# A window-attention block and a channel attention on one core: token deviations by quarter, slices turned around the third down-product, moments one product later, the attention's end in another order

## The reference, cut to what matters

```python
# first block: shifted-window attention (12 heads of 8, windows of 8 x 8), then an MLP
x = shortcut + window_attention(layernorm(x))          # over channels, per pixel
h = _layernorm(x, norm2_g, norm2_b)                    # (x - mu) * rsqrt(var + eps) * g + b, per pixel
h = jax.nn.gelu(h @ fc1_w + fc1_b, approximate=False)  # 96 -> 384
x = x + (h @ fc2_w + fc2_b)                            # 384 -> 96
# second block: channel attention; statistics over a whole image
mu = jnp.mean(x, axis=(1, 2, 3), keepdims=True)
var = jnp.mean((x - mu) ** 2, axis=(1, 2, 3), keepdims=True)
xn = (x - mu) * jax.lax.rsqrt(var + EPS) * ln_g + ln_b
Q, K, V = _proj(xn, ...)                               # 12 x 12 per head, then a 3 x 3 depthwise convolution
logits = jnp.einsum('bhnc,bhnd->bhcd', K, Q) / alpha
out = jnp.einsum('bhnc,bhcd->bhnd', V, softmax(logits))
return jnp.einsum('bcij,oc->boij', out, w_f) + b_f + xn
```

## Time and profile before

| | |
|---|---|
| time, median of 3 runs | 512.71 us (511.64 to 522.3) |
| the profiled execution's own time | 512.89 us |
| its span in the profile | 511.1 us |
| PE busy | 488.5 us, 96% of the span |
| DVE, ACT, POOL busy | 371.9, 292.6, 190.3 us |
| PE on the chain that ended last | 36% of the span, the largest share |
| mean granted clock of PE | 0.983 of full speed |

### The profile page before, as it was taken

One profiled execution on the slowest core, in us unless ns is written; L12 is line 12 of the kernel. 1 busy time (PEld: TensorE's weight loads), 2 busy tenths in 40 slices (PEclk: granted clock), 3 DMA queues, 4 the chain that ended last, 5 costly groups with the idle time before them and its releaser, 6 DMA issues. The chain is left out here.

```text
span 511.1 us, 22940 instructions
## 1 busy us (share of the span) xinstructions
PE 488.5 (96%) x8866; PEld 312.7 (61%) x8866; DVE 371.9 (73%) x1016; ACT 292.6 (57%) x740; POOL 190.3 (37%) x222
## 2 busy tenths in 40 slices
PE   7999999999999999999888997889999999999996
PEld 7777777777777777777643332325565556555563
DVE  2599999999999999998775362356776565565543
ACT  2477788777787777886564353143444444444332
POOL 8543444443434434344250413035325332332300
PEclk8899999999999999999999999889999999999998
DMA  4211011111011110100033142356543444434311
GB/s 81 64 35 33 21 26 49 31 31 27 21 31 31 31 31 21 40 1 3 3 74 74 32 99 53 82 130 150 137 128 98 127 110 117 114 103 130 106 38 34
DMA packets 41180, 32.55 MB, mean 64 GB/s; under 512 B 19240, under 2 KB 36776, under 8 KB 41128
## 3 DMA queue, kind: packets, MB, share of 16 engines
q1 hardware_dynamic: 36872, 25.36, 19.4%
q0 software_dynamic: 3584, 5.72, 5.1%
q10 hardware_dynamic: 672, 0.75, 0.5%
HBM read 18.36 MB, written 7.13 MB: 50 GB/s over the span
## 5 line engine op out<-in xcount | busy, mean ns | idle before, releaser
L379 POOL TENSOR_TENSOR scores<-scores,peak 128x768 f32<-128x768 f32 x64 | 94.2, 1472 | 129.8 <-DVE peak L548 129.8
L1033 POOL DMA_DIRECT2D x_stack<-padded_x x96 | 52.2, 547 | 95.8 <-PE ps_hidden L1552 63.6
L442 ACT COPY probs_t<-ps_probs 128x768 f32<-128x768 f32 x64 | 51.1, 798 | 40.4 <-PE ps_probs L702 40.3
L540 DVE TENSOR_TENSOR scores<-ps_scores,bias 128x768 f32<-128x768 f32 x64 | 61.3, 958 | 5.6 <-PE ps_scores L692 3.8
L548 DVE TENSOR_REDUCE peak<-scores 128x12 f32<-128x768 f32 x64 | 61.0, 953 | 2.4
L715 PE MATMUL ps_out<-v_blocks,probs_t 128*64 128x54 f32 x1536 | 57.1, 224 | 1.0 <-ACT out_t L447 0.9
L715 PEld LDWEIGHTS ps_out<-v_blocks,probs_t 128*64 128x64 f32 x1536 | 50.2, 138 | 12.3 <-issue 12.2
L436 ACT ACTIVATE scores<-scores 128x768 f32<-128x768 f32 x64 | 54.2, 847 | 1.5 <-POOL scores L379 1.5
L702 PE MATMUL ps_probs<-ident,scores 128*128 128x128 f32 x384 | 54.3, 277 | 0.0
L1140 ACT ACTIVATE hidden<-ps_hidden,fc_b_folded 128x512 f32<-128x512 f32 x44 | 26.6, 688 | 39.3 <-PE ps_hidden L1469 38.8
L1552 PE MATMUL ps_turn<-x_stack,conv_w 40*32 40x256 f32 x1536 | 48.8, 379 | 0.0
(11 more groups left out here) (159 smaller groups left out, 850.9 us busy)
## 6 DMA issues: line engine op xcount, KB each, us to landing
x_stack<-padded_x POOLq DMA_DIRECT2D x96, 54.0 KB, 2.7
x_stack<-padded_x SPq DMA_DIRECT2D x96, 54.0 KB
padded_x<-x_pad SPq DMA_DIRECT2D x26, 121.5 KB, 2.6
x_sliced<-stream SPq DMA_DIRECT2D x48, 64.0 KB, 2.0
stream<-y_sliced SPq DMA_DIRECT2D x48, 64.0 KB, 2.0
out<-out_sb SPq DMA_DIRECT2D x32, 96.0 KB, 2.2
x_now<-in_x SPq DMA_DIRECT2D x32, 72.0 KB, 1.8
stream<-in_x SPq DMA_DIRECT2D x32, 72.0 KB, 1.9
```

Of the source, the lines that this page charges most:

```text
L379: nc.gpsimd.tensor_tensor(sc, sc, peak[:, par, p, :].unsqueeze(2).to_broadcast((128, HEADS, WN)), ALU.subtract).then_inc(s["shifted"], 1)
L442: nc.scalar.copy(probs_t[:, :], ps_turned).then_inc(s["turned_copied"], 1)
L540: nc.vector.tensor_tensor(scores[:, par, p, :].rearrange("p (g c) -> p g c", g=NG), ps_scores[:, :, 0:GROUP * WN], bias[:, p, :].rearrange ...
L1033: engine.dma_start(x_stack[64 * half + i * HC:64 * half + (i + 1) * HC, slot, :, :], rows).then_inc(landed[slot], 16)
```

## The change

- **Attention's end.** PE turns chunks 4 and 5 ahead of the first fold, 6 ahead of the second, 7 after it, and does the third fold after the loop, where the 16 filling products stood. ACT takes its copies in that order. The three slice copies move from DVE to ACT, and the load of the GELU table from the end of this stage to the start of the next.
- **Deviations by quarter.** `quarter_deviation` makes shift and power for one quarter (4 columns) right ahead of that quarter's scaling, in place of one of 16 columns ahead of four scalings.
- **Turned slices.** `turn_back(g + 1, 0)` and `(g + 1, 1)` stand ahead of `down(g - 1, 2)`, `turn_back(g + 1, 2)` behind it. The turns of the third weight and of the final weight, and their copies on DVE, move from group 0 to group 1, behind its first up-product.
- **Moments.** In the last group `sum_means`, `center_means` and `sum_spreads` stand one product later; the inverse roots come in three parts of 2, 4 and 10 images, and `take_gain` of images 0 and 1 waits for the first, of 2 to 5 for the second. All six `start_image` stand behind the last GELU and ahead of the table load.

```diff
@@ window attention, ACT
             if is_image(t, B - 1):
+                copy_first(0)
                 copy_fold(0)
+                copy_first(1)
                 copy_fold(1)
-                for k in range(QUARTERS, 2 * QUARTERS):
-                    copy_tokens(nc, act, m, s2, k, by_blocks(first_homes[k - QUARTERS]))
-                    if k == QUARTERS + 1:
-                        copy_fold(2)
-                token_deviation(nc, act, m, s2, 1)
-                nc.scalar.preload_act_table_set("gelu_and_others")
+                copy_first(2)
+                copy_fold(2)
...
+        def copy_slice(c):
+
+            act.wait_ge(s2["turned_ready"], c + 1)
+            nc.scalar.copy(m["normed2"][:, c, :], ps_slices[c]).then_inc(s2["normed_ready"], 1)
...
         led_image_loop(act, step)
+        copy_slice(0)
+        copy_first(3)
+        copy_slice(1)
+        token_deviation(nc, act, m, s2, 1)
+        copy_slice(2)
...
@@ window attention, PE
             if last:
+                turn_first(QUARTERS)
+                turn_first(QUARTERS + 1)
                 fold_fc1(0)
+                turn_first(QUARTERS + 2)
                 fold_fc1(1)
-                for k in range(QUARTERS, 2 * QUARTERS):
-                    turn_first(k)
-                fold_fc1(2)
+                turn_first(QUARTERS + 3)
...
-        fill(nc, ps_out[0:C, 0, 0:C], blank[:, :], 16)
+        fold_fc1(2)
         for c in range(SLICES):
             turn_first_slice(c)
...
+def quarter_deviation(nc, pool, m, s, g, r, exponent, shifted):
+
+    n = (g - 2) * QUARTERS + r
+    pool.wait_ge(s["spread_ready"], (g * QUARTERS + r + 1) * BLOCKS)
+    need(pool, s["quarter_ready"], n)
+    need(pool, s["scaled_ready"], (g - 1) * QUARTERS + r + 1)
+    nc.gpsimd.tensor_scalar(m["log_var2"][:, r, :], m["spread_mlp"][:, r, :, 1], EPS, None, ALU.add).then_inc(shifted, 1)
+    pool.wait_ge(shifted, n + 1)
+    nc.gpsimd.tensor_tensor(m["rstd2"][:, r, :], m["log_var2"][:, r, :], exponent[:, 0:1].to_broadcast((128, BLOCKS)),
+                            ALU.pow).then_inc(s["quarter_ready"], 1)
...
@@ MLP, POOL
         for g in range(2, GROUPS):
-            token_deviation_by_power(nc, pool, m, s, g, exponent, variance_shifted)
             for r in range(QUARTERS):
+                quarter_deviation(nc, pool, m, s, g, r, exponent, variance_shifted)
                 scale_tokens(nc, pool, m, s, g, r)
...
+            for first, last in ((0, 2), (2, AHEAD), (AHEAD, EARLY)):
+                at = batch * EARLY
+                nc.gpsimd.tensor_tensor(moments[:, at + first:at + last, 0], spread2[:, first:last, 1],
+                                        exponent[0:C, 0:1].to_broadcast((C, last - first)), ALU.pow).then_inc(deviations_set, 1)
...
@@ MLP, ACT
-            if g == LAST:
-                act.wait_ge(cleared, CLEARED)
-                start_image(0)
-                start_image(1)
             gelu(g, 2)
+        act.wait_ge(cleared, CLEARED)
+        for t in range(AHEAD):
+            start_image(t)
         nc.scalar.preload_act_table_set("natural_log_exp_and_others")
-        for t in range(2, AHEAD):
-            start_image(t)
...
@@ MLP, DVE
+            if g == 1:
+                copy_weights(2, 2)
+                copy_final()
...
             if g == 0:
-                for place, kind in enumerate((1, 0, 2)):
-                    copy_weights(place, kind)
-                copy_final()
+                copy_weights(0, 1)
+                copy_weights(1, 0)
...
@@ MLP, PE
             if last:
-                sum_spreads(0)
+                sum_means(0)
             if g > 0:
                 down(g - 1, 1)
+            if last:
+                sum_spreads(0)
             up(g, 2)
-            if g > 0:
-                down(g - 1, 2)
+            if more:
+                turn_back(g + 1, 0)
+                turn_back(g + 1, 1)
             if g == 0:
-                turn_back(1, 0)
-                turn_back(1, 1)
                 turn_weights(0, 1)
                 turn_weights(1, 0)
-                turn_back(1, 2)
-                turn_weights(2, 2)
-                nc.tensor.transpose(ps_final, w["final"][:, :], ident[0:C, 0:C]).then_inc(weights_turned, 1)
-            elif more:
-                for c in range(SLICES):
-                    turn_back(g + 1, c)
+            else:
+                down(g - 1, 2)
+            if more:
+                turn_back(g + 1, 2)
```

More of the change, by code:

```diff
@@ L837, in measure_tokens @@
     dve.wait_ge(s["stats_ready"], (k + 1) * BLOCKS)
-    need(dve, s["rstd_ready"], k // QUARTERS)
+    need(dve, s["rstd_ready"], min(k // QUARTERS, 2))
+    need(dve, s["quarter_ready"], k - 3 * QUARTERS + 1)
     for b in range(BLOCKS):
@@ L1256, in center_means @@
             dve.wait_ge(means_summed, batch + 1)
-            need(dve, deviations_set, batch)
+            need(dve, deviations_set, batch * PARTS_OF_BATCH)
             nc.vector.tensor_reduce(mean_sum[:, :], sums, AX_X, ALU.add).then_inc(moments_set, 1)
@@ L1349, in _ @@
                 add_residual(g - 1, 0)
-            if last:
-                center_means(0)
             if 1 < g < LAST:
@@ L1511, in _ @@
             up(g, 0)
+            if g == 1:
+                turn_weights(2, 2)
+                nc.tensor.transpose(ps_final, w["final"][:, :], ident[0:C, 0:C]).then_inc(weights_turned, 1)
             if later:
@@ L1515, in _ @@
                 down(g - 1, 0)
-            if last:
-                sum_means(0)
             if later:
```

36 lines of the change are left out of this document (13 added, 23 removed).

## The result

The changed kernel takes 498.91 us, median of 4 runs (499.01, 507.1, 497.83, 498.81), against 515.92 us for the kernel before, median of 4 (511.64 to 522.3): a ratio of 0.9696 with a 95% interval from 0.9631 to 0.9761, faster. The ratio leaves out the execution of 507.1 us, which lies apart from the others; the experiments show what such an execution of this kernel is. The profiled execution took 499.01 us for a span of 497.2 us, at a mean granted clock of 0.994.

The account below looks back on a forecast made before the run. PE was taken as the path, with holes, up to image 2's products of the channel attention. Savings of 1.7 + 1.0 + 3.2 + 7.5 = 13.4 us from 512.9 us gave 499.5 us, range 497 to 503.5 us.

Parts of the forecast that it names:

- Part 1: Attention's end: new order of turns, folds and copies brings the last slice copy from 257.36 to 255.7 us, saving 1.7 us.
- Part 2: Group 0: PE's 1.42 us wait for turned conv weights goes as the turns move behind the next up-product, saving 1.0 us.
- The 0.4 us that were to stay: Group 0: of PE's 1.42 us wait, 0.4 us stay because the next up-product needs a GELU that ended at 268.77 us.
- Part 3: Groups 2 and 3: deviations by quarter and turned slices ahead of the down-product remove PE's waits, saving 3.2 us.
- the margin of 0.2 us: Group 3: POOL's chain ends at 306.7 us, PE asks at 306.88 us; a small power over 1.0 us costs time.
- Part 4: Last group and first images: later moment products and pads behind the GELU bring image 2 from 49.2 to 41.7 us, saving 7.5 us.
- their 0.4 us hole: Last group: PE is done at 8.3 us, moments are ready at 8.7 us, so it waits 0.4 instead of 3.19 us.
- 0.5 us for the taps to land: Between PE's last down-product at 25.6 us and the first taps' product: a wait of 0.5 us.
- SP ends last, PE waits 1.2 us: At image 2: SP's chain allows its products at 41.7 us, PE gets there at 40.5 us and waits 1.2 us.
- First rival: POOL's quarters: the small power keeps its price, every quarter costs 4.2 us, 515.0 us in all; chance 0.08.
- Second rival: MLP's start: without filler PE stands about 2 us and the clock falls, costing 1.7 us, 501.2 us; chance 0.17.
- Third rival: SP's gathers wait the full 3.4 us, image 2 comes 2.9 us later and half clock adds 1.7 us: 504.1 us; chance 0.15.

## Why the prediction was right

The forecast was 499.5 us, the profiled execution took 499.01 us. From the last heads to image 2 the sum said 13.4 us and the traces say 13.10 us (1.56 + 1.42 + 2.65 + 7.47); 1.56 us of luck in the start and 0.74 us lost at the kernel's end belong to neither.

- **Part 1,** 1.7 us: 1.56 us. The new order does it; moving the copies to ACT costs 0.16 us, which the bounds held and the sum had not named.
- **Part 2,** 1.0 us: 1.03 us, namely 1.42 us less the 0.39 us that the moved turns take in the next stretch (268.50 to 268.89). The 0.4 us that were to stay are the 0.45 us ahead of 265.71.
- **Part 3,** 3.2 us: 3.04 us (2.65 + 0.39). The power of 4 columns is 1.04 us and not 0.93 us, just over the point from which it was to cost something, but it stays hidden: shift and hand-overs are 0.07 us shorter, and of the margin of 0.2 us 0.05 us are left. With 2.93 us for 16 columns this is (2.93 - 1.04) / 12 = 0.16 us a column and 0.41 us besides. The three inverse roots of 2, 4 and 10 columns lie near the same line, at 0.69, 1.00 and 1.95 us. The Trainium skill, GPSIMD: programming the Q7 cores, section SBUF Data Layout, says that a read hands a core one vector of 16 lanes from 16 partitions, from which the prediction took a price by the column; the trace agrees for all but the 0.41 us.
- **Part 4,** 7.5 us: 7.47 us, but this is luck, two errors that cancel. PE was through 24.87 us after the first up-product, not 25.6 us, because the moments were ready at 8.14 us (311.36 + 2.71 - 305.93) and their 0.4 us hole did not come. Against that, the step "0.5 us for the taps to land" was 1.63 us, and the stretch from there to image 2 was 15.23 us and not 14.4 us, 0.40 us of it idle. The step "SP ends last, PE waits 1.2 us" failed: image 2's products have no wait ahead of them, since SP's last joins are issued by 34.34 us (331.78 + 8.49 - 305.93) and not by 37.2 us. SP matters one step earlier, with its gathers of the first taps behind its joins.
- **First rival,** the small power keeps its price: it doesn't. The run with one power isn't that case, but it shows what late scaled tokens cost: 9.9 us in two groups, with half clock behind the second hole only, where the rival had it behind both.
- **Second rival,** clock at the MLP's start: real, and seen in one of twelve profiles that have this order without filler there. The other eleven had the same hole of 1.4 to 1.7 us and kept 1.00. The Trainium skill, TensorE: Matmul & The Clock Gate, section What's actually happening, which the prediction cites there, says that half rate is the default and that activity lifts it. It follows neither from that nor from these traces that filler is needed in a stand of this length.
- **Third rival,** SP: the pads did leave ACT ahead of its table load, and twelve gathers took 5.17 us, so its wait of 3.4 us did not come.

What the prediction lacked is the third hole. It asked of three places whether the clock would fall and priced 1.7 us. At the first taps it saw 0.5 us of waiting, where 1.64 and 2.32 us came in the two profiles of the changed kernel, and with the longer one a loss of 8.3 us. The forecast is that of the executions in which this doesn't happen; that three of the first four runs were such is luck as far as the runs tell, for in the repeated runs the same kernel had a median of 507.68 us, outside the range.

## What to carry to other kernels

When an edit makes PE arrive earlier at a stage whose data come by transfers, the wait moves to the first use of that data: ask who issues these transfers and what is queued ahead of them. Here it was enough to move the one producer (a 0.41 us copy on ACT) that starts their chain; moving SP's transfers too gained nothing more. A kernel can have two times, so repeat the runs before believing a median of four, and compare the profiles of a short and a long execution stretch by stretch. Work split by columns is worth it even at a start-up price per piece, where the pieces let the order of the consumer change.

## What the hardware showed that I had not expected

- At the start of the channel attention the clock fell in all six profiles in which PE had waited 1.95 us or longer for the first taps (1.95, 2.32, 2.78, 2.79, 2.84, 3.91 us), and in none of the other six (1.64, 0.55 us and less). It stayed at 0.50 for 20.5 us in five of them and 23.9 us in the sixth, with PE busy for all of it, where the falls in the MLP lasted 3.4 or 6.8 us. In the MLP a hole of 1.69 us was followed by half clock in one profile and one of 3.41 us wasn't, so the length by itself isn't a rule.
- Two executions of one kernel, equal to 0.01 us in the stretches before, differed by 1.0 us in the time SP took to issue the same twelve joins (7.76 and 8.76 us), all of it in the twelfth (0.59 and 1.71 us), with the DMA engines' share at 0.52 and 0.57 during the joins; 8.3 us hung on it.
- A power on POOL took 2.93 us for 128x16 elements and 1.04 us for 128x4, where a shift of the same shapes took 0.26 and 0.23 us.
